# Second attention's key and value weights in a load of their own, and their products inside the first attention's first steps

## What is computed

```python
x = x + tanh(g_xattn[0]) * L0_xattn(layernorm(x), ctx, ctx, mask_bf0, Wq, Wk, Wv, Wo)   # 16 heads of 64
x = x + tanh(g_ffn[0])   * L0_ffn(layernorm(x), w_gate, w_up, w_down)                    # ternary weights
x = x + tanh(g_xattn[1]) * L1_xattn(layernorm(x), ctx, ctx, mask_ik0, w_q, w_k, w_v, w_o, b_o)   # 16 heads of 8
x = x + tanh(g_ffn[1])   * L1_ffn(layernorm(x), Wg, W1, b1, W2, b2)                      # 8 experts, top 2
...                                                                                      # two more such layers
```

## Time and profile before

| | us |
|---|---|
| median of three runs | 516.53 |
| lowest and highest | 513.0, 519.35 |
| the profiled execution, its own time | 514.63 |
| its span, first to last instruction | 512.8 |

### The profile page before, as it was taken

How to read it: one execution, slowest core, us unless ns; L and a number is a source line. 1 busy time by engine, 2 the same in 40 slices (tenths; PEclk the granted TensorE clock), 3 DMA queues, 4 the chain that set the end, 5 groups by cost and what they waited for, 6 DMA issues and landing times.

```text
span 512.8 us, 8536 instructions
## 1 busy us (share of the span) xinstructions
PE 430.0 (84%) x2872; PEld 338.2 (66%) x2886; DVE 336.4 (66%) x1001; ACT 275.1 (54%) x565; POOL 141.6 (28%) x257
## 2 busy tenths in 40 slices
PE   5799899898897789889996799727779999999733
PEld 4587787787786566667786488515556777777722
DVE  1386876886976867757876122236757677888674
ACT  3343345454455356645562265323877889888553
POOL 3180010010120222204434300078552234442252
PEclk9999999999999999979998699955999999999655
DMA  8970000000000020000000223111000000000000
GB/s 312 411 283 2 1 1 2 1 1 1 1 3 0 1 106 20 1 0 12 12 17 20 88 78 116 43 36 37 11 1 2 2 1 0 2 6 6 7 10 15
DMA packets 8570, 21.41 MB, mean 42 GB/s; under 512 B 1376, under 2 KB 4689, under 8 KB 8401
## 3 DMA queue, kind: packets, MB, share of 16 engines
q1 hardware_dynamic: 7505, 18.78, 10.3%
q0 software_dynamic: 1024, 2.10, 1.4%
HBM read 14.00 MB, written 6.88 MB: 41 GB/s over the span
## 4 chain that ended last, share of the span: by engine, by line
PE 65%; DVE 15%; ACT 7%; issue 6%; POOL 6%; DMA 2%; POOLq 0%; DVEq 0%; ACTq 0%; another core or an unknown queue 0%
PE bank L821 9%; PE bank L847 8%; PE bank L829 7%; PE bank L866 4%; PE bank L843 4%; PE bank L805 3%; PE bank L861 3%; PE bank L984 3%; PE bank L992 3%; PE bank L946 2%; PE bank L957 2%; POOL moe_rows L528 2%; PE bank L935 2%; PE bank L788 2%; DVE prob L1218 2%
## 5 line engine op out<-in xcount | busy, mean ns | idle before, releaser
L1214 DVE TENSOR_REDUCE mx<-bank 128x4 f32<-128x512 f32 x96 | 65.8, 685 | 45.3 <-PE bank L821 29.7
L479 POOL TENSOR_SCALAR rstd<-mv 128x1 f32<-128x1 f32 x48 | 10.1, 211 | 241.7 <-DVE mv L1174 240.3
L561 ACT ACTIVATE probT<-bank 128x512 f32<-128x512 f32 x96 | 56.9, 592 | 34.0 <-PE bank L829 31.7
L569 ACT ACTIVATE prob<-prob 128x512 f32<-128x512 f32 x96 | 60.0, 625 | 25.7 <-DVE prob L1218 25.1
L847 PEld LDWEIGHTS bank<-va,probT 128*128 128x128 f32 x512 | 65.8, 199 | 3.0 <-issue 2.9
L1218 DVE TENSOR_TENSOR prob<-bank,mx 128x512 f32<-128x512 f32 x96 | 65.3, 681 | 1.6 <-PE bank L829 0.3
L829 PE MATMUL bank<-pack,prob 128*128 128x128 f32 x384 | 59.8, 279 | 5.2 <-ACT sg L637 1.4
L847 PE MATMUL bank<-va,probT 128*128 128x9 f32 x512 | 63.8, 252 | 0.3
L829 PEld LDWEIGHTS bank<-pack,prob 128*128 128x128 f32 x384 | 46.7, 147 | 25.5 <-issue 22.2
L821 PE MATMUL bank<-moe_rows,qz 128*128 128x512 f32 x64 | 34.2, 618 | 0.1
L821 PE MATMUL bank<-kz,qz 128*128 128x512 f32 x64 | 32.6, 599 | 1.4 <-issue 1.4
(11 more groups left out here) (230 smaller groups left out, 944.9 us busy)
## 6 DMA issues: line engine op xcount, KB each, us to landing
yrows_d<-moe_rows SPq DMA_DIRECT2D x2, 1510.0 KB, 19.2
pack<-pack_d SPq DMA_DIRECT2D x5, 512.0 KB, 8.2
pack<-pack_d SPq DMA_DIRECT2D x1, 2112.0 KB, 14.8
expert<-experts_d SPq DMA_DIRECT2D x4, 514.0 KB, 9.2
pack<-experts_d SPq DMA_DIRECT2D x4, 514.0 KB, 4.6
xrows_d<-moe_rows SPq DMA_DIRECT2D x1, 1080.0 KB, 17.9
moe_rows<-xrows_d SPq DMA_DIRECT2D x8, 135.0 KB, 3.0
yrows_d<-o_n SPq DMA_DIRECT2D x8, 135.0 KB, 1.8
```

What stands on the lines that cost most here:

```text
L561: act.activation(dst, src, ACT.Identity if kw else ACT.Copy, **kw).then_inc(E[layer][name].sem, 1)
L569: act.activation(prob[:, g % 2, :], prob[:, g % 2, :], ACT.Exp, scale=float(DK0 if layer == A0 else DK) ** -0.5).then_inc(E[layer]["probs" ...
L1214: yield from do(dve.tensor_reduce(m, src, AX.X, ALU.max))
```

## The change

The 512 columns of `wkT_1`, `wkT_3` and `wvT_13` go to the end of `pack0`. The first load stops ahead of x and them, x keeps its place, and the 512 columns come in a load of their own with the semaphore `kv_loaded`, issued between the value and the output weights. The four pieces `kv(0, c)` leave TensorE's `prepare` and become `early_kv`, one in each slot of step 0, with ScalarE's part in `early_kv_sb`. They use banks 2 to 5 now (`KV_BANK`); the fourth attention's pieces keep banks 0 to 3. `banks_free` goes; the first transposes and value products of item 0 wait for `kv_act` instead. The bank table of A0 gets a name, `AT0`, and one entry of it differs: the second key half, `k1`, is in bank 7 (was 6), for every item.

```diff
-PACK_FIRST = dict(ctxT=N, wkT_1=P, wkT_3=P, wvT_13=2 * P, ident=P, ones=P, causal=P, hmask=GH, bk_3=1, bq_3=1, gates=8, x=N)
+PACK_FIRST = dict(ctxT=N, ident=P, ones=P, causal=P, hmask=GH, bk_3=1, bq_3=1, gates=8, x=N, wkT_1=P, wkT_3=P, wvT_13=2 * P)
...
+AT0 = dict(xt=0, k0=0, k1=1, q0=1, q1=1, v0=0, v1=0, ot0=1, ot1=1, y=1, q=1, ot=0)
...
+        KV_BANK = (T_BANK + O_BANK, S_BANK + T_BANK)
...
-            cut = sum(PACK_FIRST.values()) - N
+            end = sum(PACK_FIRST.values()) - 4 * P
+            cut = end - N
...
-            sp.dma_start(packed[0][:, cut:], packs[0][:, cut:]).then_inc(loaded[5], 16)
+            sp.dma_start(packed[0][:, cut:end], packs[0][:, cut:end]).then_inc(loaded[5], 16)
             load_att0(1)
             sp.dma_start(mask0_u8[:, :, :], mask0_d).then_inc(mask0_loaded, 16)
             load_att0(2)
+            sp.dma_start(packed[0][:, end:], packs[0][:, end:]).then_inc(kv_loaded, 16)
             load_att0(3)
...
             def prepare():
                 act.wait_ge(loaded[0], 16)
                 act.activation(tanh_g[:, :], col["gates"], ACT.Tanh).then_inc(gates_ready, 1)
-                for c in range(4):
+
+            def early_kv_sb(it, c):
+                if it.rep == 0:
                     kv_sb(0, c)
...
-                    return R_BANK[{"xt": 0, "k0": 0, "k1": 0, "q0": 1, "q1": 1, "v0": 0, "v1": 0, "ot0": 1, "ot1": 1,
-                                   "y": 1, "q": 1, "ot": 0}[piece]]
+                    return R_BANK[AT0[piece]]
...
+                if layer == A0 and it.rep == 0 and g < 2:
+                    pe.wait_ge(kv_act, g + 1)
...
+                    if it.rep == 0 and g < 2:
+                        pe.wait_ge(kv_act, g + 3)
...
-                for c in range(4):
+
+            def early_kv(it, c):
+                if it.rep == 0:
+                    pe.wait_ge(kv_loaded, 16)
                     kv(0, c)
-
-            def banks_free():
-                pe.wait_ge(kv_act, 4)
...
-                     [(1, probsT, A0, 1), (0, proj0, 'v', 1), (0, proj0, 'q', 1), (1, pv, A0, 0)]],
+                     [(1, probsT, A0, 1), (0, proj0, 'v', 1), (0, proj0, 'q', 1), (0, early_kv, 3), (1, pv, A0, 0)]],
```

More of the change, by code:

```diff
@@ L307, in build @@
         rows_loaded, mask0_loaded, mask1_loaded = sem("rows_loaded"), sem("mask0_loaded"), sem("mask1_loaded")
-        lens_loaded = sem("lens_loaded")
+        lens_loaded, kv_loaded = sem("lens_loaded"), sem("kv_loaded")
         expert_loaded = [sem(f"expert_loaded{e}") for e in range(NE)]
@@ L578, in k_sb @@
                 wait(act, A0, "kps", it, c + 1)
-                evac(kz[:, it.k, 512 * c:512 * c + 512], bank[R_BANK[0]][:, :], A0, "k_sb")
+                evac(kz[:, it.k, 512 * c:512 * c + 512], bank[R_BANK[AT0[f"k{c}"]]][:, :], A0, "k_sb")
             def q_sb0(it, c):
                 wait(act, A0, "qps", it, c + 1)
-                evac(qT[:, it.k, 512 * c:512 * c + 512], bank[R_BANK[1]][:, :], A0, "q_sb")
+                evac(qT[:, it.k, 512 * c:512 * c + 512], bank[R_BANK[AT0[f"q{c}"]]][:, :], A0, "q_sb")
             def q_sb(it, layer):
@@ L683, in kv_sb @@
                 if c < 2:
-                    act.activation(kT[:, half, :].rearrange("p b t -> p (b t)"), bank[c][:, :],
+                    act.activation(kT[:, half, :].rearrange("p b t -> p (b t)"), bank[KV_BANK[n][c]][:, :],
                                    ACT.Identity if kw else ACT.Copy, **kw).then_inc(kv_act, 1)
                 else:
-                    act.activation(va[:, half, :, 0:DK], bank[c][:, :].rearrange("p (b h n) -> p b h n", b=4, h=H),
+                    act.activation(va[:, half, :, 0:DK], bank[KV_BANK[n][c]][:, :].rearrange("p (b h n) -> p b h n", b=4, h=H),
                                    ACT.Copy).then_inc(kv_act, 1)
@@ L712, in _ @@
             stages = {
[L713 to L716, removed]
+                A0: [[(2, exps, A0, 3), (2, probsT_sb, A0, 2), (0, k_sb, 0), (0, early_kv_sb, 0)],
+                     [(1, exps, A0, 0), (2, probsT_sb, A0, 3), (0, k_sb, 1), (0, early_kv_sb, 1)],
+                     [(0, xt_sb, A0), (1, exps, A0, 1), (1, probsT_sb, A0, 0), (0, q_sb0, 0), (0, early_kv_sb, 2)],
+                     [(1, exps, A0, 2), (1, probsT_sb, A0, 1), (0, q_sb0, 1), (0, early_kv_sb, 3)]],
                 F0: [[(1, up_sb)], [], [None, None, (0, xq_sb, F0), (1, hq_sb, F0)], [None, (0, half_gate)]],
@@ L1006, in kv @@
                 first = 4 * (c % 2)
-                out = bank[c]
+                out = bank[KV_BANK[n][c]]
                 if c < 2:
@@ L1073, in _ @@
             stages = {
-                A0: [[(1, row_scores0, 0), (2, probsT, A0, 2), (3, ot0, 1), (2, pv, A0, 1), (0, proj0, 'k', 0)],
-                     [(2, probsT, A0, 3), (0, proj0, 'k', 1), (3, y0), (2, pv, A0, 2), (0, xt, A0), (2, ot0, 0)],
-                     [(1, probsT, A0, 0), (1, row_scores0, 1), (0, proj0, 'v', 0), (0, proj0, 'q', 0), (2, pv, A0, 3)],
-                     [(1, probsT, A0, 1), (0, proj0, 'v', 1), (0, proj0, 'q', 1), (1, pv, A0, 0)]],
+                A0: [[(1, row_scores0, 0), (2, probsT, A0, 2), (3, ot0, 1), (2, pv, A0, 1), (0, proj0, 'k', 0), (0, early_kv, 0)],
+                     [(2, probsT, A0, 3), (0, proj0, 'k', 1), (3, y0), (2, pv, A0, 2), (0, xt, A0), (2, ot0, 0), (0, early_kv, 1)],
+                     [(1, probsT, A0, 0), (1, row_scores0, 1), (0, proj0, 'v', 0), (0, proj0, 'q', 0), (0, early_kv, 2), (2, pv, A0, 3)],
+                     [(1, probsT, A0, 1), (0, proj0, 'v', 1), (0, proj0, 'q', 1), (0, early_kv, 3), (1, pv, A0, 0)]],
                 F0: [[(2, y_ffn, F0, tern['downT']), (1, up, F0, 'up', tern['upT'][:, :], xqT)],
@@ L1124, in note @@
             def note(layer, fn, it, *args):
+                if fn is early_kv:
+                    return
                 if fn is row_scores0:
@@ L1136, in _ @@
             walk(pe, PLAN, stages,
-                 before={(MOE, 0): kv3, (A0, 3): weight_sums, (F0, 0): ternary_ready(3), (A0, 1): banks_free, (A2, 0): fold,
+                 before={(MOE, 0): kv3, (A0, 3): weight_sums, (F0, 0): ternary_ready(3), (A2, 0): fold,
                          (F2, 0): lambda: pe.wait_ge(fold_dve, FT + 1)})
@@ L1225, in v_sb @@
                 wait(dve, A0, "pv", it.back(2), 2 * c + 2)
-                dve.tensor_copy(va0[:, it.k, 8 * c:8 * c + 8, 0:DK0], bank[R_BANK[0]][:, :].rearrange(
+                dve.tensor_copy(va0[:, it.k, 8 * c:8 * c + 8, 0:DK0], bank[R_BANK[AT0[f"v{c}"]]][:, :].rearrange(
                     "p (h n) -> p h n", h=8)).then_inc(E[A0]["v_sb"].sem, 1)
@@ L1232, in ot_sb0 @@
                     wait(dve, A0, "y", it.back(2))
-                dve.tensor_copy(oT[:, it.k, 512 * c:512 * c + 512], bank[R_BANK[1]][:, :]).then_inc(E[A0]["ot_sb"].sem, 1)
+                dve.tensor_copy(oT[:, it.k, 512 * c:512 * c + 512], bank[R_BANK[AT0[f"ot{c}"]]][:, :]).then_inc(E[A0]["ot_sb"].sem, 1)
             def norm0(it, g):
```

## The result

The changed kernel takes 519.13 us (median of 20 runs, 515.27 to 524.4); the kernel before, run beside it, 514.05 (20 runs, 511.11 to 520.35). The ratio is 1.008, with a 95% interval of 1.0054 to 1.0106: slower by 0.8%, which is less than 2% but clear of no change. Ratios and intervals here leave out the slow executions, over 1.5% above the fastest of their kernel (four of the 20 before, three of the 20 changed), so they aren't the quotients of the medians. The profiled execution took 516.86 us for a span of 515.0.

A forecast was written before the change was run, and what follows sets the result against it. TensorE was taken to bound the kernel (430.0 of 512.8 us busy, 65% of the chain). Terms 3.1 - 0.3 - 0.25 + 0.6 gave +3.1 us: 517.7 or 519.6 by scale, predicted 518.5, range 514 to 522.5.

The forecast's parts named there:

- The load, the stand and the half pace: Run-up: new load lands at about 12.0, TensorE stands from 8.7 until then and begins again at half pace.
- the 2.9 in the sum: Run-up: slow start of TensorE, 2.94 us in the old kernel's kv pieces, moves behind the stand at the same cost.
- rival A: Run-up: TensorE at full pace when the load lands, scores at 20.6, sum +0.2, time 516 us; chance 20%.
- A kv piece covers the evacuation of x: Run-up: a kv piece on TensorE hides the evacuation of the transposed x, whose old stand was 0.29 us.
- all three stands of the old run-up: TensorE's stands for evacuating the first key half (0.61), the second (0.60) and transposed x (0.29 us), forecast gone.
- The bank: Second key half in bank 7: step 1 gains 0.3 us, step 2 0.25, step 4 loses 0.6, others swallow it.
- Rival C: Steps 3 to 7: bank 7's 0.6 us delay is not swallowed, 2.4 us more, 520.9 us; chance 14%.
- Rival B: Run-up: kv weights land by about 8.7, no stand, scores at 19.2, 514.5 us between the scales; chance 6%.
- Rival D: Run-up: new load lands at 13.0 or more, 519.5 us, or 521.5 with landing at 15; chance 10%.
- The scale: Whole kernel: 517.7 us from the profiled execution, 519.6 from the three-run median 516.53; 518.5 chosen between.

The follow-up runs named there:

- kv_load_2nd: Changed kernel with the new load issued right behind the first key weights instead of behind the value weights; ratio to the kernel before 1.0103, median 518.99 us.
- warm_fill: Changed kernel with three more 128x512 matmuls, result overwritten, one before the first key half and two behind it; ratio to the kernel before 1.004, median 516.78 us.
- bank_back: Changed kernel with the second key half back in bank 6; ratio to the kernel before 1.0192, median 523.17 us.
- xt_first: Changed kernel with ScalarE's second key evacuation placed behind that of the transposed x; ratio to the kernel before 1.0083, median 518.34 us.
- bank_only: Kernel before with only the first attention's second key half moved from bank 6 to bank 7; ratio 0.999, median 513.78 us.
- repaired: Changed kernel with the edits of kv_load_2nd and xt_first, and bank 7 for the second key half in steps 0 to 2 only; ratio to before 0.9968.
- late_kv: The four key and value pieces moved to steps 3, 5, 6, 7, load last, bank 7 in steps 0 to 2 only; ratio to the kernel before 1.0002.
- late_kv_ln: As late_kv, with VectorE doing item 0's layernorm ahead of the first mask; ratio to the kernel before 0.9911, median 510.85 us.

## Why the prediction was right, and where it was not

The forecast was 518.5 (514 to 522.5); measured 519.13. From the traces: +3.1 us forecast for the first attention, +3.5 measured. That 518.5 came so near has luck in it, as the last paragraph of this section shows.

**The load, the stand and the half pace: right.** 11.95 forecast, 11.73 measured; the first matmul at 6.8 (6.85); a stand of 3.3 us (2.84, because the key half at half pace took 2.05); the pieces at 1061 ns behind it. kv_load_2nd shows that the load's place in the queue makes the stand, and warm_fill that the stand's second price is the pace: 2.55 us less with the pieces at full pace, against the 2.9 in the sum. So the reading in which work ahead of the stand counts (rival A) is not how the changed kernel went: in both its traces, in bank_back and in xt_first TensorE came out of the stand at half pace.

**"A kv piece covers the evacuation of x": wrong.** This is the step that failed: the sum held that all three stands of the old run-up were gone, and one came back, worth 0.94 us. I looked at TensorE's order only. ScalarE's order puts the evacuation of x behind that of the same kv piece, so the piece delays it instead of covering it; xt_first removes the stand. The load came 0.3 earlier, and the half pace cost 2.7 instead of 2.94 (the three pieces behind the load took 2.08 + 1.71 + 1.72 in the chain, where I had 0.95 + 0.89 + 0.95 at full pace). This and some tenths of overlap hide most of the fault in the sum: 23.5 forecast, 23.74 measured. That they cancel is luck. The sum was built on the chain's rows and compared with 20.37 there; the chain has 23.91, so like with like it is 0.4 short, the same 0.4 as between +3.1 and +3.5.

**The bank.** Step 1 forecast -0.3, measured -0.23; step 2 -0.25, measured -0.52 (the stand of 0.25 counts from the modelled end of the transposes; from start to start the second key half follows them by 0.85 us before and 0.43 after, which is 0.4, and the last 0.1 comes right behind it; bank_only and bank_back show the same size); step 4 +0.6, measured +0.71; steps 3 and 5 to 7 swallowed it, as said. In step 1 TensorE stood twice for ScalarE before (0.69 and 0.78) and stands 1.01 for VectorE's layernorm now. bank_only and bank_back give the same three numbers from both sides. Rival C falls: 0.78 us of standing in each of five steps cost 0.7 in one.

**Rival B** (faster, with the weights there before 8.7) was tried by kv_load_2nd: even with the load at 7.5 the start (21.13) is no better than before (20.20), since the layernorm is next (1.75) and the stand of 0.95 stays. The prediction has no term for the layernorm; the stand for the load hid it. (The "half a megabyte" in the rival is a slip: the load has 256 KB.) **Rival D** falls with the landing at 11.7.

**The scale.** The 516.53 of the three runs was 2.5 above the median of 20, 514.05. On that the sum would have given 517.2, 1.9 below what was measured; the ratio's interval is 2.8 to 5.4 us. So a scale that was 2.5 too high made up for a sum that was 1 to 2 us too low: that part of the hit is luck. The sum of the parts in the traces, 3.5, lies inside the interval. If the other trace of before is taken, it is 4.8 to 4.9. Which is typical is open: there are two traces of each kernel. (bank_only, whose first pieces are the same as before, has the early pace as well.)

## What to carry to other kernels

A wait for a load in an in-order engine's program costs what stands behind it, so a piece that nobody needs soon belongs where its engine stands anyway, not at the first place where a bank is free. When a piece is put between two others on one engine, look at where its evacuation lands in the next engine's program. A stand in TensorE's first microseconds may be paid twice, as time and as half pace after it; and once one stand is mended, look for the next engine (here VectorE, with a mask ahead of a layernorm) before counting the gain.

## What the runs showed of the hardware

**TensorE starts at half pace, and reached full pace late where it had stood.** The same 128x512 instruction took 1061 ns and 592, a ratio of 1.8, so these are the clock's two levels, 1.2 and 2.4 GHz. In every trace TensorE began slowly. It was at full pace by 9.0 and near 11.4 in two executions of the kernel before, which works from 5.5 on without a stand until then; at 18.4 in the changed one, with a stand of 2.84 us; near 24.6 in bank_back, with stands of 2.76, 0.78 and 0.95; by 8.2 in warm_fill. Once TensorE was up, a stand of 1.75 us (kv_load_2nd) or 1.81 (warm_fill) left it at full pace, and one of 2.31 (repaired) was followed by half pace. These are single traces, and xt_first, which did the same as the changed kernel up to there, was up at 15.3; the tests of the stands themselves are warm_fill, which fills them, and bank_back, which adds one. The row of a window gives a granted clock of 1.00 all the while the earlier trace rows, also while the durations are those of half pace, so at a kernel's start the durations tell what that column doesn't.

**The second attention took up to 8 us more or less from one execution to the next.** Windows from 165 to 240 us (length, engines' busy times, granted clock, DMA share, GB/s), first the two executions of the kernel before:

```profile
165.00:240.00 75.00, 65.05 (x416) 50.17 (x418) 54.37 (x148) 38.84 (x88) 15.53 (x27) 0.95 0.07 24
```

```profile
165.00:240.00 75.00, 64.72 (x365) 49.39 (x368) 49.43 (x137) 34.63 (x76) 12.49 (x25) 0.84 0.07 22
```

then warm_fill and late_kv:

```profile
165.00:240.00 75.00, 64.83 (x364) 48.87 (x365) 47.76 (x128) 34.15 (x75) 10.98 (x20) 0.84 0.06 22
```

```profile
165.00:240.00 75.00, 65.07 (x426) 49.68 (x429) 56.49 (x159) 40.38 (x91) 15.84 (x29) 0.98 0.07 24
```

At a mean granted clock of 0.84 TensorE is as busy (64.7 us) but gets through 365 matmuls where it does 416 at 0.95 and 426 at 0.98. From the scores of step 8 to the first expert's transpose the traces have 154.2 us in both executions at 0.84, 147.5 at 0.95 and 145.7 at 0.98. That is 8 us, more than the whole change, and 6.6 of them lie between the two executions of the kernel before. What decides it I haven't found. It is nearly as large as the scatter of single executions (511 to 520 us in the kernel before), so one execution can hide a start gain of 2.5 us.

That a shorter start is lost there for good is not shown, and the ratios speak against it. By the scores of step 8 late_kv_ln is 4.1 to 5.3 us ahead of the two traces of the kernel before, and by its ratio 4.6 us faster; the changed kernel is 3.5 to 4.9 behind and 4.1 slower; bank_back 7.1 to 8.3 behind and 9.9 slower. kv_load_2nd (0.9 to 2.1 behind, 5.3 slower) and xt_first (1.4 to 2.7 behind, 4.3 slower) fit worst, but their intervals begin at 1.2 and 1.5 us.
